# A three-stage macaron layer on one core: batches written out, side jobs spread over all sixteen slots, x2 begun on GpSimd

## The chip, the core and the metric

The kernel runs on one core of a Trainium2 chip. The metric is the device time of one execution in microseconds (us), the lower the better. The engines are TensorE (PE: matmuls; its weight loads are listed as PEld), VectorE (DVE), ScalarE (ACT), GpSimd (POOL) and SyncE (SP, which here only issues DMAs). Each runs its own list of instructions in order; semaphores tie them together.

## What is computed

Eight batches of 512 rows by 256 columns pass three steps, all in float32:

```python
x = x + 0.5 * ffn(layernorm(x), w_re, w_im, bias)
x = x + attn(layernorm(x), Wq, Wk, Wv, Wo, bo)
x = x + 0.5 * ffn(layernorm(x), w_re, w_im, bias)

def ffn(x, w_re, w_im, bias):      # FFT over 256, times a complex 256x256 matrix, inverse FFT
    y = real(ifft(fft(x) @ complex(w_re, w_im)))
    return y + bias

def attn(x, Wq, Wk, Wv, Wo, bo):   # only the left 128 columns enter; 16 heads of 8
    left = x[..., :128]
    q, k, v = (left @ W.T for W in (Wq, Wk, Wv))        # each (512, 16, 8)
    att = softmax(q k^T / 4)                            # 16 x 512 x 512 per batch
    return (att v) @ Wo.T + bo
```

## The kernel before, in words

The FFT, the matrix and the inverse FFT are linear, so a **prologue** folds them once into one real 256x256 matrix, `half_ffn`: six products with cosine and sine tables on TensorE (`spectral`, L504), put together on VectorE (`fold`, L859 and L860). After that each batch has a prefix, an attention and a suffix.

The **attention** of a batch is 16 *slots* (`QUADS`). In slot s TensorE makes the scores of four heads for one block of 128 keys, in two pairs (`score_pair`, L587: stationary `KS`, moving `QS`, 34 rows deep); ScalarE takes the exponent of each pair, 128x1024 at a time (L489); and `value_quad` (L606) multiplies `VS` with the four heads' `probs`, side by side in four column groups of the array, 32 wide each. The code issues the scores of slot s+1, then the `value_quad` of slot s, then the jobs of slot s. There are two score banks, so a pair waits until ScalarE has read the pair two before it. After slots 0 to 7 and 8 to 15 `normalize` (L778 to L789) divides by the sums of the exponents; its second call ends in `otn`.

Around these lie small **jobs** on TensorE, each evacuated by VectorE, in two shared PSUM banks (`misc`) in turn, so a job waits until the job two before it has been evacuated. The prefix of a batch is F1_0 to F1_3 (first FFN, four row tiles, L529, to `x1`), LT (transposes of the normalised left half `lh`, L561), KT, QT and V (projections), N and NT (a bound on the scores: squares on GpSimd, summed and transposed, L570 to L574). The suffix is WO_0 to WO_3 (output projection, added to `x2`), T3_0 and T3_1 (transposes of `x2`, L546) and F2_0 to F2_3 (second FFN, to `x_out`). `x2` begins as `x1` plus `bo` (`begin_x2`, L793, VectorE); `x_in` and `x_out` get the bias on GpSimd (`add_bias`, L409), and `rstd_of` (L404, L406) makes the reciprocal standard deviations there. Tables at the top of the file (`PREFIX`, `SUFFIX`) say in which slot a job goes: while batch b is in its slots, the suffix of b-1 and the prefix of b+1 are done.

`KT` and `QT` are split in two parts (`split`, L718 and L720, to `kp` and `qp`), **stored to DRAM and read back as stacked rows** (`stack_parts`, L312 to L332): 8 DMAs of 128 KB each for `KS` and 8 for `QS`, on SP. The `guard` reads one number on TensorE and VectorE (L613, L800); where it says that the scores are small, a long block is jumped over and the shift rows are zero. Four small DMAs then put them into `QS` (L340; L481 on ScalarE's queue for the first batch).

Batches 0 and 7 are written out; batches 1 to 6 are three rounds of a hardware loop of two batches on each engine. `keep_awake` (L511) are matmuls on zeros that fill waits of TensorE in the prologue and after the last batch.

## Time and profile before

| | us |
| --- | --- |
| time before, median of 3 runs | 401.53 (400.44 to 403.65) |
| the profiled execution | 399.26 |
| its span, first to last instruction | 397.5 |
| PE busy / ACT busy / DVE busy / POOL busy | 363.7 / 248.4 / 196.4 / 92.3 |
| granted TensorE clock, mean | 0.983 |

The span is shorter than the time of the same execution by what lies around the first and last instruction (1.8 us). Busy time of PE includes the modelled ends of pipelined matmuls, so 92% is not 92% of its peak. A slot is best read from the start of one `value_quad` to the start of the next in the PE timeline; a batch from the start of its slot 0 (47.43 us for batch 0, 83.24 for batch 1, 347.63 for batch 7).

### The profile page before, as it was taken

How to read it: one execution, taken by the hardware profiler on the slowest of the kernel's cores; microseconds unless marked ns; L12 is line 12 of the kernel's file. 1: busy time of each engine (PE TensorE's matmuls, PEld its weight loads, DVE VectorE, ACT ScalarE, POOL GpSimd, SP SyncE). 2: the span in 40 equal slices, each digit the busy share in tenths (PEclk: the TensorE clock that was granted, in tenths of full speed). 3: DMA queues.
4: the chain of work that ended last, by engine and by line, in shares of the span. 5: the costliest groups of instructions: out<-in, count | busy, mean ns of one | idle time of the engine just before them, and what ended most of it. 6: DMA issues, size and time to landing. Idle time of an engine off the chain costs nothing.

```text
span 397.5 us, 9585 instructions
## 1 busy us (share of the span) xinstructions
PE 363.7 (92%) x3436; PEld 142.1 (36%) x3441; DVE 196.4 (49%) x511; ACT 248.4 (62%) x261; POOL 92.3 (23%) x96
## 2 busy tenths in 40 slices
PE   5887599999999999899999999899999999999986
PEld 3734133233333333233333333233433333333323
DVE  1575243246645575156645575427554673333354
ACT  1100378967686767737676767736687667887730
POOL 6351120402430131302430141301530131003004
PEclk9999899999999999989999999969999999999999
DMA  8509939500874039230874039230781038200001
GB/s 220 160 0 230 202 115 162 156 2 2 197 132 160 2 128 178 81 109 2 200 129 160 2 140 177 68 108 2 186 142 54 2 128 178 77 2 2 27 28 53
DMA packets 19500, 40.75 MB, mean 103 GB/s; under 512 B 3504, under 2 KB 6064, under 8 KB 18416
## 3 DMA queue, kind: packets, MB, share of 16 engines
q1 hardware_dynamic: 17968, 39.27, 40.2%
q10 hardware_dynamic: 1472, 0.67, 0.8%
q8 instruction: 39, 0.64, 0.7%
q14 instruction: 21, 0.17, 0.2%
HBM read 26.69 MB, written 12.58 MB: 99 GB/s over the span
## 4 chain that ended last, share of the span: by engine, by line
PE 73%; issue 9%; ACT 8%; DVE 4%; DMA 3%; ACTq 2%; DVEq 0%; POOL 0%
PE ot L606 25%; PE misc L529 22%; PE scores L587 19%; ACT probs L489 8%; PE misc L546 2%; PE scores L504 2%; DMA cos_var_sb<-cos_var 2%; DMA QS<-shift 1%; PE misc L561 1%; ACTq L481 1%; PE scores L511 1%; DVE kp L718 1%; DVE kp L720 1%; DVE stats L689 0%; ACTq L266 0%
## 5 line engine op out<-in xcount | busy, mean ns | idle before, releaser
L489 ACT ACTIVATE probs<-scores 128x1024 f32<-128x1024 f32 x256 | 245.6, 1024 | 119.1 <-PE scores L587 118.9
L606 PE MATMUL ot<-probs,VS 128*32 128x512 f32 x1024 | 139.0, 615 | 0.3 <-ACT probs L489 0.3
L587 PE MATMUL scores<-QS,KS 34*128 34x512 f32 x512 | 105.3, 467 | 18.4 <-ACT probs L489 9.5
L587 PEld LDWEIGHTS scores<-QS,KS 34*128 34x128 f32 x512 | 42.4, 186 | 99.0 <-ACT probs L489 68.0
L404 POOL TENSOR_SCALAR veps<-mv 128x4 f32<-128x4 f32 (+1 forms) x25 | 6.6, 263 | 236.9 <-DVE mv L696 236.9
L744 DVE SCALAR_TENSOR_TENSOR x_out<-misc,rstd,x_out 128x256 f32<-128x256 f32 x32 | 15.5, 483 | 50.9 <-PE misc L529 50.7
L529 PE MATMUL misc<-half_ffn,xT_in 128*32 128x256 f32 x512 | 33.3, 397 | 3.6 <-issue 2.3
L606 PEld LDWEIGHTS ot<-probs,VS 128*32 128x32 f32 x1024 | 20.3, 108 | 42.4 <-issue 40.5
L529 PE MATMUL misc<-half_ffn,xT 128*32 128x256 f32 x512 | 33.0, 379 | 0.4 <-DVE xT L729 0.4
L735 DVE SCALAR_TENSOR_TENSOR x<-misc,rstd,x_in 128x256 f32<-128x256 f32 x32 | 15.5, 484 | 30.6 <-PE misc L529 30.2
L529 PEld LDWEIGHTS misc<-half_ffn,xT_in 128*32 128x32 f32 x512 | 17.6, 115 | 23.3 <-issue 13.7
L406 POOL TENSOR_TENSOR rstd<-veps,power 128x4 f32<-128x4 f32 (+1 forms) x25 | 25.3, 1011 | 2.1
L689 DVE BATCH_NORM_STATS2 stats<-x 128x6 f32<-128x256 f32 x64 | 25.1, 415 | 0.0
L529 PEld LDWEIGHTS misc<-half_ffn,xT 128*32 128x32 f32 x512 | 16.7, 110 | 23.2 <-issue 15.6
L729 DVE COPY xT<-misc 128x512 f32<-128x512 f32 x16 | 11.0, 691 | 22.7 <-PE misc L546 22.7
L739 DVE TENSOR_TENSOR x<-misc,x 128x256 f32<-128x256 f32 x32 | 13.5, 423 | 17.5 <-PE misc L529 17.4
L529 PE MATMUL misc<-wo_sb,otn 128*32 128x256 f32 x256 | 19.4, 380 | 0.8 <-DVE otn L789 0.7
L409 POOL TENSOR_TENSOR x_out<-x,half_bias 128x1024 f32<-128x1024 f32 (+1 forms) x9 | 19.1, 2127 | 0.0
L415 POOL TENSOR_TENSOR sq_k<-kp 128x512 bf16<-128x512 f32 x8 | 8.3, 1040 | 46.1 <-DVE kp L718 46.1
L409 POOL TENSOR_TENSOR x_in<-x_in,half_bias 128x1024 f32<-128x1024 f32 x8 | 19.0, 2377 | 0.0
L689 DVE BATCH_NORM_STATS2 stats<-x_in 128x6 f32<-128x256 f32 x32 | 11.2, 414 | 15.1 <-DMA x_in<-x 7.6
L778 DVE STREAM_TRANSPOSE ot_t<-ot 128x512 f32<-128x512 f32 x16 | 11.4, 710 | 13.4 <-PE ot L606 13.2
(77 smaller groups left out, 240.4 us busy)
## 6 DMA issues: line engine op xcount, KB each, us to landing
KS<-k_scr SPq DMA_DIRECT2D x64, 128.0 KB, 4.6
QS<-q_scr SPq DMA_DIRECT2D x64, 128.0 KB, 4.8
x_in<-x SPq DMA_DIRECT2D x8, 512.0 KB, 4.2
xT_in<-x_t SPq DMA_DIRECT2D x8, 512.0 KB, 4.9
k_scr<-kp SPq DMA_DIRECT2D x8, 512.0 KB, 2.7
q_scr<-qp SPq DMA_DIRECT2D x8, 512.0 KB, 3.4
out<-x_out SPq DMA_DIRECT2D x14, 256.0 KB, 2.1
out<-x_out SPq DMA_DIRECT2D x4, 128.0 KB, 1.9
```

The costliest lines, as they stand in the source:

```text
L406: nc.gpsimd.tensor_tensor(rstd[k][:, tiles], veps[k][:, tiles], power[:, tiles], ALU.pow).then_inc(rstd_done[k], 1)
L409: nc.gpsimd.tensor_tensor(dst[:, tiles, :], src[:, tiles, :], half_bias[:, :].unsqueeze(1).to_broadcast([P, tiles.stop - tiles.start, E]), ...
L489: nc.scalar.activation(probs[u % PRING][:, :, :], scores[u % 2][:, :, :], ACT.Exp, scale=SCORE_SCALE).then_inc(exp_done, 1)
L529: last = mm(dst[cols, :], lhsT[:, cols], rhs, start=c == 0, stop=c == len(terms) - 1)
L587: last = mm(scores[u % 2][:, i, :], KS[par][rows, slot, kt * P:(kt + 1) * P].bitcast(F32R), QS[par][rows, slot, :].bitcast(F32R), start=Tr ...
L606: last = mm(ot[g][COL * j:COL * (j + 1), :], VS[par][:, kt, h, :], probs[(2 * s + j // 2) % PRING][:, j % 2, :], start=s % 8 == 0, stop=s ...
L689: ins = nc.vector.bn_stats(stats[k][:, t, :], src[:, t, :])
L729: nc.vector.tensor_copy(xT[:, 2 * i:2 * i + 2, :, :], bank[:, :].rearrange("p (t c q) -> p t c q", t=2, c=C)).then_inc(evacuated, 1)
L735: nc.vector.scalar_tensor_tensor(x1[par][:, i, :], tile, rstd[0][:, i:i + 1], x_in[par][:, i, :], ALU.mult, ALU.add).then_inc(evacuated, 1)
L739: nc.vector.tensor_tensor(x2[:, i, :], tile, x2[:, i, :], ALU.add).then_inc(evacuated, 1)
L744: nc.vector.scalar_tensor_tensor(x_out[:, i, :], tile, rstd[2][:, i:i + 1], x_out[:, i, :], ALU.mult, ALU.add).then_inc(evacuated, 1)
L778: nc.vector.transpose(ot_t[:, :, :].rearrange("p c r -> p (c r)"), ot[g][:, :]).then_inc(ot_taken, 1)
```

## The change

The loop is gone: every engine's list is written out for all eight batches, and waits compare with constants. One table `STEADY` takes the place of `PREFIX` and `SUFFIX` (with `BEGIN` for batch 0 and `END` for batch 7). In it QT, V, N and NT belong to the next batch, but F1, LT and KT to the batch after that (+2). For this there are three `x1` buffers, the `left_half` (to `lh`) is written in slot 11, and `kp` is stored a batch ahead (`k_out`). `x2` is begun on GpSimd, after the previous batch's T3_1 and its `x_out`. The guard stands after the jobs of slot 10; the first `normalize` in slot 12.

`k_scr` is laid out as `q_scr` was, and rows in `KS` are ordered by part first; a `QS` DMA now writes 32 rows (256 KB) from a source read twice, so a batch has 8 DMAs for `KS` and 4 for `QS`.

In the prologue the cosine table with row 0 zeroed is loaded whole, and the plain low half (`cos_low`) after the bias on ScalarE's queue; the identity and small weights come on SP behind batch 0's `x`; `bo` and `wo` come last. The exponent table is loaded early by a small activation. NT of batch 0 stands ahead of V; of batch 1 only F1_0 and F1_1 are done there. The stacked rows of batch 0 are issued from SP and ScalarE, for the first eight slots; those for the last eight slots wait for `rest_wanted`, set by TensorE when it starts on the scores. After the last batch the transposes go to score banks and are copied by ScalarE, between the WO and F2 jobs.

```diff
-PREFIX = {0: ["F1_0", "F1_1"], 1: ["F1_2", "F1_3"], 3: ["LT"], 4: ["KT"], 5: ["QT"], 6: ["V"], 7: ["N"], 8: ["NT"]}
-SUFFIX = {3: ["WO_0"], 4: ["WO_1"], 5: ["WO_2"], 6: ["WO_3"], 8: ["T3_0"], 9: ["T3_1"],
-          11: ["F2_0"], 12: ["F2_1"], 13: ["F2_2"], 14: ["F2_3"]}
-GUARD_SLOT = 9
-NORM0_SLOT = 10
...
+STEADY = {0: [("QT", 1)], 1: [("V", 1)], 2: [("WO_0", -1), ("N", 1)], 3: [("WO_1", -1), ("NT", 1)],
+          4: [("WO_2", -1), ("WO_3", -1)], 5: [("T3_0", -1), ("T3_1", -1)],
+          6: [("F1_0", 2)], 7: [("F1_1", 2)], 8: [("F1_2", 2)], 9: [("F1_3", 2)],
+          10: [("F2_0", -1)], 11: [("F2_1", -1)], 12: [("F2_2", -1)], 13: [("F2_3", -1)],
+          14: [("LT", 2)], 15: [("KT", 2)]}
+BEGIN = {0: [("F1_2", 1)], 1: [("F1_3", 1)], 3: [("LT", 1)], 4: [("KT", 1)], 5: [("QT", 1)], 6: [("V", 1)],
+         7: [("N", 1)], 8: [("NT", 1), ("F1_0", 2)], 9: [("F1_1", 2)], 10: [("F1_2", 2)], 11: [("F1_3", 2)],
+         14: [("LT", 2)], 15: [("KT", 2)]}
+END = {2: [("WO_0", -1)], 3: [("WO_1", -1)], 4: [("WO_2", -1)], 5: [("WO_3", -1)], 6: [("T3_0", -1)],
+       7: [("T3_1", -1)], 9: [("F2_0", -1)], 10: [("F2_1", -1)], 11: [("F2_2", -1)], 12: [("F2_3", -1)]}
+GUARD_SLOT = 10
+LEFT_SLOT = 11
...
-        x1 = [sb(f"x1_{i}", [P, T, E]) for i in range(2)]
+        x1 = [sb(f"x1_{i}", [P, T, E]) for i in range(3)]
...
+        def k_rows(eng, par, g, side):
+            heads = slice(HEADS * side + 4 * g, HEADS * side + 4 * (g + 1))
+            for j in range(PARTS):
+                first = SIDE * side + PARTS * Dh * j
+                eng.dma_start(KS[par][first:first + PARTS * Dh, 4 * g:4 * (g + 1), :],
+                              k_scr[j, :, heads, :].unsqueeze(0).to_broadcast([PARTS, Dh, 4, S])).then_inc(rows_loaded[g], 16)
+
+        def q_rows(eng, par, g, side):
+            heads = slice(HEADS * side + 4 * g, HEADS * side + 4 * (g + 1))
+            eng.dma_start(QS[par][SIDE * side:SIDE * side + SROW, 4 * g:4 * (g + 1), :],
+                          q_scr[:, :, heads, :].rearrange("i d h s -> (i d) h s").unsqueeze(0)
+                          .to_broadcast([PARTS, PARTS * Dh, 4, S])).then_inc(rows_loaded[g], 16)
...
+            def first_rows():
+
+
+                sp.wait_ge(evacuated, evac_count("KT", 0))
+                store_k(sp)
+                sp.wait_ge(k_stored, 16)
+                k_rows(sp, 0, 0, 0)
+                sp.wait_ge(q_stored, 16)
+                q_rows(sp, 0, 0, 0)
+                sp.wait_ge(rest_wanted, 1)
+                for side in range(SIDES):
+                    k_rows(sp, 0, 1, side)
+                for side in range(SIDES):
+                    q_rows(sp, 0, 1, side)
...
+            def rows_in(b):
+                sp.wait_ge(evacuated, evac_count("QT", b))
+                store_q(sp)
+                wait(sp, quad_done, QUADS * (b - 1))
...
+            for it in range(B):
+                if it == 0:
+                    load_x(2)
+                    k_out(1)
+                if it + 1 < B:
+                    rows_in(it + 1)
+                if it + 3 < B:
+                    load_x(it + 3)
+                if it + 1 < B:
+                    shift_rows(it + 1)
+                if it >= 1:
+                    store_out(it - 1)
+                if it + 2 < B:
+                    k_out(it + 2)
...
+            def end_of(b):
+                rstd_of(2, b + 1)
+                wait(pool, out_stored, 32 * b)
+                add_row(x_out, x2, half_bias, x2b_done)
+
+            def begin_x2(b):
+
+                pool.wait_ge(evacuated, evac_count("F1_3", b))
+                if b >= 1:
+                    pool.wait_ge(evacuated, evac_count("T3_1", b - 1))
+                    pool.wait_ge(x2b_done, b)
+                add_row(x2, x1[b % 3], bo_sb, x2_begun)
+
...
+            for it in range(1, B):
+                if it + 1 < B:
                     square(qp, sq_q, qp_step, it + 1)
+                end_of(it - 1)
+                begin_x2(it)
+                if it + 2 < B:
+                    rstd_of(1, it + 3)
+                if it + 3 < B:
+                    next_x(it + 3)
+                if it + 2 < B:
+                    square(kp, sq_k, kp_step, it + 2)
+            pool.wait_ge(out_stored, 32 * (B - 1))
             for i in range(2):
+                pool.wait_ge(evacuated, evac_count(f"WO_{2 * i + 1}", B - 1))
+                add_row(x_out, x2, half_bias, x2b_done, slice(2 * i, 2 * i + 2))
                 rstd_of(2, B + i, slice(2 * i, 2 * i + 2))
...
+            act.wait_ge(waking_set, 1)
+            nc.scalar.activation(probs[0][:, 0, 0:32], waking[:, 0:32], ACT.Exp, scale=SCORE_SCALE)
...
+            act.wait_ge(k_stored, 16)
+            k_rows(act, 0, 0, 1)
+            act.wait_ge(evacuated, evac_count("QT", 0))
+            store_q(act)
+            act.wait_ge(q_stored, 16)
+            q_rows(act, 0, 0, 1)
             act.wait_ge(shift_ready, 1)
             for side in range(SIDES):
...
+            pe.sem_inc(rest_wanted, 1)
...
+            def last_transposes(i):
+                pe.wait_ge(evacuated, evac_count(f"WO_{2 * i + 1}", B - 1))
+                transpose_x2(scores[0][:, i, :], i).then_inc(lastT_ready, 1)
+
+            job("WO_0", B - 1)
+            job("WO_1", B - 1)
+            job("WO_2", B - 1)
+            last_transposes(0)
+            job("WO_3", B - 1)
+            job("F2_0", B - 1)
+            last_transposes(1)
+            job("F2_1", B - 1)
+            job("F2_2", B - 1)
+            job("F2_3", B - 1)
 
 
         @block.vector
         def _(dve):
...
+            def left_half(b):
+                dve.wait_ge(rstd_done[1], b + 1)
+                for t in range(T):
+                    last = nc.vector.tensor_scalar(lh[:, t, :], x1[b % 3][:, t, 0:HD], mv[1][:, t, 0:1],
+                                                   rstd[1][:, t:t + 1], ALU.subtract, ALU.mult)
...
-            def begin_x2(par):
-
-                nc.vector.tensor_tensor(x2[:, :, :], x1[par][:, :, :], bo_sb[:, :].unsqueeze(1).to_broadcast([P, T, E]),
-                                        ALU.add).then_inc(x2_begun, 1)
-
...
+            for it in range(B):
                 for s in range(QUADS):
-                    if s == 0 and not is_first(it):
-                        begin_x2(1 - par)
+                    if s == 0 and it >= 1:
                         normalize(it - 1, 1)
-                    run_jobs(it, par, s)
-                    if s == 9:
+                    run_jobs(it, s)
+                    if s == 2 and it == 0:
+                        left_half(1)
+                    if s == 5 and it == 0:
+                        norm0_stats(2)
+                        norm_moments(0, 3)
+                    if s == GUARD_SLOT and it + 1 < B:
+                        guard(it + 1)
+                    if s == LEFT_SLOT and it + 2 < B:
+                        left_half(it + 2)
+                    if s == 12:
                         normalize(it, 0)
-                    if s == GUARD_SLOT and not is_last(it):
-                        guard(it + 1)
-                    if s == NORM0_SLOT and tail:
-                        norm0_moments(it + 2, par)
-
-            body(0, 0)
-            with dve.Fori(1, B - 3, 2) as i:
-                body(i, 1)
-                body(i + 1, 0)
-            for it in range(B - 3, B):
-                body(it, it % 2, tail=it + 2 < B)
-            dve.wait_ge(evacuated, ring_base(EPILOGUE))
-            begin_x2((B - 1) % 2)
+                    if s == 13 and it + 3 < B:
+                        norm0_stats(it + 3)
+                        norm_moments(0, it + 4)
```

**TensorE, batches in the middle.** First the kernel before, slots 2 and 3 of a batch (`wo_sb,otn` is WO, `ident,lh` is LT):

```order
L606 MATMUL ot<-probs,VS 32x512 x4
L266 REGISTER_ALU
L587 MATMUL scores<-QS,KS 128x512 x2
L266 REGISTER_ALU
L587 MATMUL scores<-QS,KS 128x512 x2
L606 MATMUL ot<-probs,VS 32x512 x4
L266 REGISTER_ALU
L529 MATMUL misc<-wo_sb,otn 32x256 x4
L266 REGISTER_ALU x2
L561 MATMUL misc<-ident,lh 128x128 x4
```

and slots 2 and 3 after the change (`sq` rows are N, `ident,norms` is NT):

```order
L629 MATMUL ot<-probs,VS 32x512 x4
L546 MATMUL misc<-wo_sb,otn 32x256 x4
L594 MATMUL misc<-sq_q,head_ones 32x512
L595 MATMUL misc<-sq_k,head_ones 32x512
L611 MATMUL scores<-QS,KS 128x512 x4
L629 MATMUL ot<-probs,VS 32x512 x4
L546 MATMUL misc<-wo_sb,otn 32x256 x4
L598 MATMUL misc<-ident,norms 1x64
L611 MATMUL scores<-QS,KS 128x512 x4
```

Slot 2 had nothing between its `value_quad` and the next scores; now it has WO_0 and N, and the register instructions are gone.

**VectorE, the turn of a batch.** Before, where a batch begins (`x_0` is x1):

```order
L793 TENSOR_TENSOR x<-x_0,bo_sb 128x1024
L266 ISA
L778 STREAM_TRANSPOSE ot_t<-ot 128x512
L266 ISA
L780 RECIPROCAL recip<-ot_t 128x32
L266 ISA
L783 TENSOR_TENSOR on<-ot_t,recip 128x16x16
L266 REGISTER_ALU
L789 STREAM_TRANSPOSE otn<-on 128x512
L266 ISA
L266 REGISTER_ALU
L735 SCALAR_TENSOR_TENSOR x_0<-misc,rstd,x_in 128x256
```

and after the change:

```order
L751 CAST kp<-misc 128x512
L753 TENSOR_TENSOR kp<-misc,kp 128x512
L810 STREAM_TRANSPOSE ot_t<-ot 128x512
L812 RECIPROCAL recip<-ot_t 128x32
L815 TENSOR_TENSOR on<-ot_t,recip 128x16x16
L821 STREAM_TRANSPOSE otn<-on 128x512
L751 CAST qp<-misc 128x512
L753 TENSOR_TENSOR qp<-misc,qp 128x512
L791 COPY VS<-misc 128x32x8 x2
L775 TENSOR_TENSOR x<-misc,x 128x256
L796 TENSOR_REDUCE norms<-misc 64x1
```

`begin_x2` is gone from this place; KT's split stands ahead of the four instructions of `normalize`, QT's split and V's copy behind them, and then the first WO and N.

**ScalarE's list in the prologue.** Before:

```order
L472 COPY even<-scores 128x258 x2
L475 ACTIVATE even<-scores 128x258
L475 ACTIVATE odd<-scores 128x258
L481 DMA QS<-shift 1x8x512 x4
L489 ACTIVATE probs<-scores 128x1024 x32
```

and after:

```order
L487 ACTIVATE odd<-scores 128x258
L277 DMA KS<-k_scr 16x1x2048 x2
L270 DMA q_scr<-qp 128x2x512
L282 DMA QS<-q_scr 32x1x2048
L289 DMA QS<-shift 1x8x512 x4
L504 ACTIVATE probs<-scores 128x1024 x256
```

Two `KS` DMAs, the store of `qp` and one `QS` DMA now stand ahead of the four shift DMAs in this list, and the store of `qp` behind the two `KS` DMAs.

## Rows read from the trace of the kernel before

**Rows 1.** Busy time by stretch: batches 0, 1, 6 and 7 (columns in the first line).

```profile
core 0: us, PE busy (x) PEld busy (x) DVE busy (x) ACT busy (x) POOL busy (x), PEclk, DMA share, GB/s
47.43:83.24 35.81, 33.97 (x251) 10.59 (x249) 11.82 (x27) 30.09 (x33) 6.58 (x5) 0.96 0.58 135
83.24:125.86 42.62, 41.12 (x418) 15.72 (x417) 24.35 (x65) 30.73 (x33) 10.59 (x10) 1.00 0.43 91
...
305.13:347.63 42.50, 41.20 (x418) 15.73 (x416) 22.40 (x56) 30.72 (x33) 6.95 (x7) 1.00 0.35 90
347.63:381.11 33.48, 32.07 (x283) 11.16 (x281) 10.47 (x24) 28.19 (x30) 3.61 (x3) 1.00 0.05 17
```

**Rows 2.** Busy time by stretch, one slot each, around batch 4.

```profile
212.73:215.12 2.39, 1.97 (x15) 0.53 (x13) 2.28 (x4) 2.39 (x3) 0.00 (x0) 1.00 0.58 158
218.50:221.88 3.38, 3.38 (x46) 1.49 (x44) 1.64 (x5) 1.94 (x3) 0.00 (x0) 1.00 0.00 0
...
226.95:229.90 2.95, 2.95 (x30) 0.97 (x28) 1.81 (x4) 1.95 (x3) 0.00 (x0) 1.00 0.00 0
...
236.11:238.49 2.38, 2.13 (x17) 0.64 (x15) 1.52 (x6) 2.38 (x3) 1.96 (x3) 1.00 0.66 195
238.49:240.93 2.44, 2.44 (x20) 0.95 (x18) 0.75 (x2) 1.43 (x3) 1.64 (x1) 1.00 0.75 134
...
243.31:245.55 2.24, 1.97 (x14) 0.53 (x12) 1.40 (x4) 2.06 (x3) 0.00 (x0) 1.00 1.07 158
245.55:248.08 2.53, 2.53 (x31) 0.98 (x29) 1.82 (x9) 1.69 (x3) 0.00 (x0) 1.00 1.06 186
```

**Rows 3.** PE timeline inside the last of these slots (start, duration, line).

```profile
246.44 1.05 PE L529 MATMUL misc<-half_ffn,xT 128*32 128x256 f32 x16
247.41 0.73 PE L587 MATMUL scores<-QS,KS 34*128 34x512 f32 x4
```

**Rows 4.** Busy time by stretch: two slots at the end of batch 0.

```profile
79.20:83.24 4.04, 3.76 (x27) 1.06 (x25) 1.04 (x2) 3.76 (x5) 0.00 (x0) 1.00 0.00 0
```

**Rows 5.** PE timeline at the loop's jump back before batch 3.

```profile
169.59 1.22 PE L587 MATMUL scores<-QS,KS 34*128 34x512 f32 x4 [2.15 <-issue]
```

**Rows 6.** PE timeline of the prologue (in brackets idle time before, and what ended it).

```profile
1.19 3.60 PE L511 MATMUL ot<-waking 128*128 128x512 bf16 x8 [1.19 <-DVE waking L863]
7.83 0.80 PE L504 MATMUL scores<-cos_var_sb,wre_sb 128*128 128x129 f32 x2 [3.05 <-DMA cos_var_sb<-cos_var]
...
17.25 3.66 PE L529 MATMUL misc<-half_ffn,xT_in 128*32 128x256 f32 x64 [1.34 <-DVE half_ffn L860]
...
44.18 0.73 PE L587 MATMUL scores<-QS,KS 34*128 34x512 f32 x4 [2.02 <-DMA QS<-shift]
```

**Rows 7.** Busy time by stretch in the prologue.

```profile
7.80:10.00 2.20, 2.17 (x10) 2.17 (x11) 0.24 (x1) 0.04 (x1) 0.88 (x1) 1.00 1.05 382
12.30:14.00 1.70, 1.70 (x16) 1.70 (x16) 0.19 (x2) 0.37 (x1) 1.70 (x2) 1.00 1.11 322
...
35.80:39.50 3.70, 3.65 (x60) 2.15 (x60) 2.12 (x5) 0.00 (x0) 0.00 (x0) 1.00 1.01 192
```

**Rows 8.** DVE timeline: the last instruction of KT's split.

```profile
28.74 0.69 DVE L720 TENSOR_TENSOR kp<-misc,kp 128x512 fp32r<-128x512 f32 x1
```

**Rows 9.** ACT timeline: the issues of the shift rows of batch 0.

```profile
35.80 3.41 ACTq L481 DMA_DIRECT2D QS<-shift  x4
```

**Rows 10.** DMA issues from 29 to 45 us (KB each, median us to landing).

```profile
KS<-k_scr SPq DMA_DIRECT2D x8, 128.0 KB, 4.6
...
k_scr<-kp SPq DMA_DIRECT2D x1, 512.0 KB, 2.7
```

**Rows 11.** PE and DVE timeline of the tail.

```profile
386.88 2.76 PE L511 MATMUL scores<-waking 128*128 128x512 bf16 x11
...
394.67 0.48 DVE L744 SCALAR_TENSOR_TENSOR x_out<-misc,rstd,x_out 128x256 f32<-128x256 f32 x1 [0.38 <-PE misc L529]
```

**Rows 12.** DVE and POOL timeline: end of `normalize`, and the bias of `x_in`.

```profile
215.47 0.71 DVE L789 STREAM_TRANSPOSE otn<-on 128x512 f32<-128x512 f32 x1
...
249.62 2.39 POOL L409 TENSOR_TENSOR x_in<-x_in,half_bias 128x1024 f32<-128x1024 f32 x1
```

More of the change, by code:

```diff
@@ new lines, with slots_of @@
+PROLOGUE, EPILOGUE = -1, B
+def slots_of(it):
+    if it == PROLOGUE:
+        return {0: [(f"F1_{t}", 1) for t in range(T)], 1: [("LT", 1)],
+                2: [("KT", 1), ("QT", 1), ("N", 1), ("NT", 1)], 3: [("V", 1), ("F1_0", 2), ("F1_1", 2)]}
+    if it == EPILOGUE:
+        return {0: [(f"{kind}_{t}", -1) for kind in ("WO", "F2") for t in range(T)]}
+    table = BEGIN if it == 0 else END if it == B - 1 else STEADY
+    return {s: [(name, d) for name, d in jobs if it + d < B] for s, jobs in table.items()}
@@ L117, in quad_units, with evac_count, jobs_at @@
+ORDER = [(it, s, name, it + d) for it in range(PROLOGUE, EPILOGUE + 1)
+         for s, jobs in sorted(slots_of(it).items()) for name, d in jobs]
+INDEX = {(name, b): n for n, (_, _, name, b) in enumerate(ORDER)}
+def evac_count(name, b):
+    return INDEX[name, b] + 1
+def jobs_at(it, s):
+    return [(name, b) for at, slot, name, b in ORDER if (at, slot) == (it, s)]
 def quad_units(s):
@@ L262, in wait @@
         def wait(eng, s, value):
[L264 to L282 removed]
+            if value > 0:
+                eng.wait_ge(s, value)
@@ L446, in _ @@
[L446 to L452 removed]
+            square(kp, sq_k, kp_step, 1)
+            square(qp, sq_q, qp_step, 1)
+            next_x(2)
+            pool.wait_ge(late_loaded, 32)
+            begin_x2(0)
+            rstd_of(1, 3)
+            next_x(3)
+            square(kp, sq_k, kp_step, 2)
@@ L490, in body @@
                                          scale=SCORE_SCALE).then_inc(exp_done, 1)
-            iterations(act, body)
+            for i in range(2):
+                act.wait_ge(lastT_ready, i + 1)
+                nc.scalar.copy(xT[:, 2 * i:2 * i + 2, :, :],
+                               scores[0][:, i, :].rearrange("p (t c q) -> p t c q", t=2, c=C)).then_inc(lastT_copied, 1)
         @block.tensor
@@ L833, in run_jobs, with last_jobs @@
                         norm_moments(k, b + 1)
-                        if kind == "F1" and not (static(it) and it == PROLOGUE):
-                            norm_apply(1, src, lh, HD, b + 1)
-            def last_suffix():
-                b, jobs, base = B - 1, [job[1] for job in LAST], ring_base(EPILOGUE)
-                def take(name):
-                    evacuate(name, jobs.index(name), base, b, b % 2, EPILOGUE)
+            def last_jobs():
+                b = B - 1
                 for i in range(2):
```

526 lines of the change are left out of this document (218 added, 308 removed).

## The prediction

> **What bounds the kernel now.** I read the page first (TensorE is busy 92% of the span), then the busy time by stretch, batch by batch, then the TensorE timeline slot by slot. A batch in the middle takes 42.5 to 42.6 us, while batch 0 takes 35.8 and batch 7 takes 33.5 [rows 1]: those two carry fewer jobs. The slots tell why. A slot with one F2 job lasts 2.53 us, with TensorE busy for all of it [rows 2]; the job itself takes 0.97 us, from its start to the next scores [rows 3], so **scores and values alone are 1.56 us of TensorE work**. Two F1 jobs make 3.38 [rows 2], so 0.91 each. WO and KT together make 2.95 [rows 2]; KT has F2's size (0.97), which leaves 0.42 for WO. T3 and NT add 0.88 [rows 2].
>
> An empty slot lasts 2.39, not 1.56, with ScalarE busy throughout; the N slot 2.38 [rows 2]. There TensorE waits for two exponents. Where several light slots follow one another, as at the end of batch 0, two last 4.04, so 2.02 each [rows 4]. Hence the limit of a slot: the larger of TensorE's work and about 2.0 us, or 2.4 for the first light slot after full ones. **Each empty slot between full ones wastes 0.8 us of TensorE.** The guard stands in an otherwise empty slot of 2.24 [rows 2]: 1.56 plus 0.68, covered by the exponents only in part.
>
> Batches 1 to 6 last 347.63 - 83.24 = 264.4 us [rows 1], against 6 x 42.5 = 255.0 for clean ones. The other 9.4 us lie mostly at the loop's two jumps back, where TensorE idles 2.15 us for nothing but instructions [rows 5], and then does the next jobs more slowly. At the ends, scores start at 44.18, after a wait for the shift rows [rows 6], and the last result is written at 394.67 + 0.48 = 395.15 [rows 11], 14 us after the last values.
>
> **Middle batches (1 to 5).** By the new table, with the prices above: QT and V slots 2 x 2.53; WO_0 with N 2.38 (N's slot alone is 2.38 by ScalarE's limit [rows 2], and I take it that WO's 0.42 fits into TensorE's wait there); WO_1 with NT 2.2; WO_2 with WO_3 2.5; both T3 2.9; four F1 slots 4 x 2.53, single ones priced as F2; F2_0 with the guard 1.56 + 0.97 + 0.68 = 3.2, since a job there no longer lets exponents cover the guard; three F2 slots 7.6; LT 2.4 (light, between full ones); KT 2.53. Sum 40.9, so -1.7 for a batch, **-8.5 for five**. If the guard's read hides behind the queued F2 matmuls, it is -2.2 a batch.
>
> **Batch 6** has no F1, LT and KT any more: four empty slots in a row, 2.38 + 3 x 2.02, take the place of four at 2.53, and slots 14 and 15 become 2.38 and 2.02. That is 38.7, or **-3.8** against 42.5. Empty slots still cost 2 us each, which is why the work it loses (some 5.4 us) does not all come back.
>
> **Batch 0** takes that work: six F1, LT and KT of batch 2. Slots by the same prices, the first 1.2 longer, since TensorE starts at the lower clock (batch 0 has 0.96 granted on the mean, and 0.04 of 35.8 us is 1.4): 3.7, 2.53, 2.38, 2.27, 3 x 2.53, 2.3, 2.73, 2.53, 3.2, 2.53, 2.38, 2.02, 2.27, 2.53. Sum 41.0, so **+5.2**. **Batch 7** keeps its jobs, each moved by a slot: 0.
>
> **The loop** goes, and with it its 9.4 us: **-9.4**. Batches 0 and 7 are written out already and show slots of the same length as in the loop, so the register instructions that go too are worth nothing.
>
> **Prologue.** The first product waits for the third table until 7.83; the waking matmuls before it take 3.60 for eight [rows 6]. Now only the first table is needed, which lands earlier, and nine waking matmuls end at about 5.2: -2.6. From 7.80 to 10.00 ten matmul rows take 2.2 us, from 12.30 to 14.00 sixteen take 1.7 [rows 7], about twice as fast, although the granted clock is printed as 1.00 in both (the level of 2.4 GHz). TensorE had idled 3.05 us before the slow ones [rows 6]; without that gap I take most of them at the fast rate, -1.6 more. So F1 starts at 13.0 instead of 17.25 [rows 6], and KT's split, which ends at 28.74 + 0.69 = 29.43 [rows 8], at 25.2. If they stay slow, it is only -2.4. The store of `kp` lands 2.7 later [rows 10], 27.9. Now SP and ScalarE issue two `KS` DMAs each, and ScalarE the store of `qp` behind its two (28.8); queued behind their data it lands at about 33, and the two `QS` DMAs, with 4.6 us as for a `KS` DMA [rows 10], at 37.6. The shift DMAs follow in ScalarE's list: four took 3.41 us to issue, from 35.80 [rows 9], and the last was waited for until 44.18, behind the rows for both halves. The second half's rows now come after, so the last shift row should land 1 to 2 us after its issue: **38.2, so -6.0**. V and two F1 fit into that time and cost nothing. Bounds: 35 (-9), if `qp` is stored as fast as `kp`; 44 (0), if rows take as long as before.
>
> Here a rule weighs against the change. From 35.80 to 39.50 the DMA engines are full (share 1.01) at 192 GB/s [rows 7]: the queue is not what is short. The Trainium skill ("Trainium Kernel Development and Optimization", Key Constraints) says that DMAs of all queues run on the same 16 engines and that issuing from several saves only issue time; the trace agrees. By that rule alone, three issues fewer in a row would be all the gain, some 1.5 us on top of the earlier start. My sum does not rest on two queues, but on half the rows being left for later.
>
> **Tail.** Eleven waking matmuls, 2.76 us [rows 11], fill the time until the last sums of `x2` are normalised, then come transposes, copies and all F2. Now the first half's transposes go ahead of WO_3, ScalarE copies them, F2_0 follows. VectorE still has its 4 sums, 4 statistics and 4 results; I get the last result at 392.4 in the old time, **-2.7** (bounds 0 and -3.5).
>
> **x2 on GpSimd.** VectorE loses one pass a batch, which TensorE never waited for: 0. GpSimd gains one pass of 2.4 us, the length of the `x_in` pass [rows 12], between slots 6 and 9; WO needs it eight slots later: 0. With the cover gone it would be 2.4 a batch. The `KS` and `QS` rows of a batch are issued from slot 0 instead of slot 5, and the shift rows one job later, still three slots ahead of use: 0. Four `QS` DMAs fewer on SP: 0.
>
> **Sum.** -8.5 - 3.8 + 5.2 - 9.4 - 6.0 - 2.7 = **-25.2**. The profiled execution took 399.26, so 374.1. It lies 2.3 below the median of the three runs shown and 1.2 below the lowest. I add half of the 2.3 and round up, since plans with tight turns seldom lose nothing: **376**.
>
> **Rivals.**
>
> 1. *The turn of a batch becomes a chain.* Before, `normalize` ended at 216.18 [rows 12], 2.6 us after the last values, with only F1 behind it. Now KT's split stands ahead of it, QT's split and V's copy behind it; WO_0 needs QT's bank, N needs V's and GpSimd's square of QT. From the start of slot 15's values: values 0.9, KT 0.97, its split 1.4 (2 x 0.69 [rows 8]), `normalize` 2.3, QT's split 1.4, so 7.0; WO_0 is due after three slots and the values, 2.53 x 3 + 0.9 = 8.5. That leaves 1.5, and with V's copy 0.9 before N. GpSimd's pass over `x_in`, 2.39 us [rows 12], ends just before. If it comes late by over 0.9 us, TensorE waits 1 to 2.4 us in each of six batches: +6 to +14, so 382 to 390. The Trainium skill ("SBUF — State Buffer", "SBUF: two separate sides") has a rule for it: a VectorE instruction with two SBUF inputs and a GpSimd one that reads SBUF lock each other out for the whole instruction. In `normalize` the product of `ot_t` and `recip` is such an instruction; no row here shows it beside a GpSimd pass.
> 2. *The rows come no sooner.* The DMA engines are full, and the store of `qp` is beside and behind four `KS` DMAs: scores start near 43, +5: 381.
> 3. *Written-out code is slower.* If TensorE's instructions were fetched too slowly wherever no loop repeats them, each block would cost what the jump back costs, 2.15 us idle [rows 5] and as much again for the slow jobs after. It decides from seven blocks on, 7 x 4 = 28 us; with ten it is +40 - 25, so 416. Against it: batches 0 and 7 are written out, and no slot there waits for instructions.
> 4. *More than forecast:* rows at 35, the guard hidden: 376 - 3 - 2.5 = 370.
>
> **Chances.** Forecast 0.58 (own range 372 to 380.5), rival 1 0.18, rival 2 0.11, rival 4 0.09, rival 3 0.04. The range for 8 in 10 is 369 to 386: it leaves out rival 3, the upper part of rival 1 and little below. About 1% (4 us) is what the runs of this kernel can tell from no change. Faster by over 1% needs under 397.5: all cases but rival 3, 0.95. Within 1%: 0.01. Slower: 0.04.
>
> **What would show each step.** Slots of a middle batch: 40.9 us from slot 0 to slot 0, no slot empty, slot 10 about 3.2, no idle time of TensorE before WO_0 and N in slot 2. Batch 0 near 41, batch 6 near 38.7, no idle for instructions above 0.7. F1 at 13.0, scores at 38.2, the last result 11.3 us after the last values start. The forecast is wrong if the idle time before TensorE's WO, N or LT jobs comes back in each batch with VectorE or GpSimd as its cause, or if middle batches stay above 42.

## The result, and the profile after

The changed kernel takes **526.18 us** (median of 4 executions, 525.09 to 527.34) against 401.02 for the kernel before in the same comparison: a ratio of 1.311, 95% interval 1.304 to 1.317. The forecast was 376 with a range of 369 to 386, so both the size and the sign are wrong. Where the executions of a kernel fell into a faster and a slower group, the time given below is that of the faster one. The profiled execution took 527.34, with a span of 525.5 and a mean granted clock of 0.844 (before: 0.983).

The page of the profile after, sections 1 to 3: busy time of each engine, the span in 40 slices, the DMA queues.

```profile
PE 369.9 (70%) x3424; PEld 141.6 (27%) x3428; DVE 178.2 (34%) x494; ACT 251.7 (48%) x264; POOL 110.3 (21%) x104
...
PE   7840698500999169952999089933998399719996
...
PEclk9995599855899769995899669985999599955999
DMA  8121413131214212230213211320212021210011
...
q1 hardware_dynamic: 14298, 38.35, 20.6%
...
KS<-k_scr SPq DMA_DIRECT2D x62, 128.0 KB
QS<-q_scr SPq DMA_DIRECT2D x31, 256.0 KB
x_in<-x SPq DMA_DIRECT2D x8, 512.0 KB, 29.6
```

No engine has added work that would explain 125 us: TensorE is busy for 369.9 us against 363.7, ScalarE for 251.7 against 248.4, GpSimd for 110.3 against 92.3 (`x2`), VectorE for less. TensorE stands still in a hole once a batch, and after each hole the clock is low. The DMA line looks idle, with 1 to 3 tenths in most slices. Yet an `x_in` load takes 29.6 us from issue to landing (median); in the kernel before it took 4.2. Full queues and idle-looking engines at the same time are what has to be explained.

Idle time of TensorE, grouped by what it waited for (us in total, times, longest):

```profile
PE scores L611 <- issue: 104.6, 6, 31.5
PE scores L611 <- DMA QS<-shift: 33.7, 2, 20.0
```

All eight large waits stand before the first scores of a batch. The jobs that rival 1 feared for (WO, N) wait for nothing in the middle batches. Busy time by stretch, from slot 0 to slot 0: batches 0, 1, 2, 6, 7, with the columns of [rows 1].

```profile
59.56:136.65 77.09, 42.81 (x359) 14.46 (x357) 21.50 (x62) 30.14 (x33) 14.15 (x13) 0.75 0.25 82
136.65:194.48 57.83, 42.38 (x418) 16.14 (x416) 21.79 (x62) 31.07 (x33) 13.05 (x12) 0.85 0.25 84
194.48:252.46 57.98, 42.45 (x419) 16.14 (x417) 21.70 (x62) 31.07 (x33) 12.99 (x12) 0.85 0.23 84
422.13:474.52 52.39, 38.12 (x343) 13.60 (x341) 14.61 (x37) 30.82 (x33) 7.83 (x6) 0.86 0.19 73
474.52:511.53 37.01, 35.93 (x282) 11.86 (x281) 9.35 (x24) 28.55 (x30) 5.99 (x4) 0.87 0.04 15
```

The hole of batch 1, in the PE timeline, and the stretches around it (slot 14's wait, slot 15, the next slot 0):

```profile
188.74 1.22 PE L611 MATMUL scores<-QS,KS 34*128 34x512 f32 x4 [15.45 <-issue]
189.90 1.93 PE L629 MATMUL ot<-probs,VS 128*32 128x512 f32 x8
191.60 1.93 PE L546 MATMUL misc<-leftT,wk_sb 128*32 128x512 f32 x8
```

```profile
171.64:187.00 15.36, 1.65 (x14) 0.58 (x12) 0.38 (x2) 1.82 (x2) 0.00 (x0) 0.68 0.23 87
...
189.90:194.48 4.58, 4.58 (x22) 1.09 (x20) 0.84 (x2) 1.79 (x3) 2.41 (x2) 0.52 0.00 0
194.48:197.00 2.52, 2.52 (x22) 0.72 (x21) 2.42 (x5) 1.89 (x3) 0.94 (x1) 1.00 0.44 171
```

After 15.45 us without work TensorE is granted 0.52 of its full clock (the level of 1.2 GHz) for the 4.58 us of slot 15, which has KT; the next slot, with as many matmuls for QT, takes 2.52 once 1.00 is granted again. So a hole costs its length and some 2.1 us more. The label "issue" is to be read with care: the matmul waits for the rows and the shift rows together, and nothing on an engine released it. The issues of SP tell the rest:

```profile
141.36 2.52 SPq L277 DMA_DIRECT2D KS<-k_scr  x4
143.93 1.31 SPq L282 DMA_DIRECT2D QS<-q_scr  x2
145.28 4.23 SPq L277 DMA_DIRECT2D KS<-k_scr  x4
149.56 7.01 SPq L282 DMA_DIRECT2D QS<-q_scr  x2
156.61 4.51 SPq L297 DMA_DIRECT2D x_in<-x  x1
161.16 0.43 SPq L298 DMA_DIRECT2D xT_in<-x_t  x1
164.70 8.39 SPq L289 DMA_DIRECT2D QS<-shift  x4
```

All of these are issued by 173.1, and the first scores start at 188.74, 47.4 us after the first row was issued. A busy stretch in between, with nothing but stacked rows under way:

```profile
150.00:155.00 5.00, 5.00 (x52) 2.33 (x54) 1.77 (x3) 3.68 (x5) 4.66 (x4) 1.00 0.12 52
```

**DMA share 0.12 of 16 engines is two engines, both full.** The packet records of the trace show the same: two packets are in flight for 4.89 of these 5 us, and three for 0.10. They move 52 GB/s here (55 and 56 in the stretches on either side). The rows of a batch are 8 x 128 KB and 4 x 256 KB, 2.1 MB: 37 us at 56 GB/s. Behind them in the same queue come `x_in`, `xT_in` and last the shift rows, of which these two engines carry their part as well. The packets show it: 112 of the 128 packets of `x_in` move between 161 and 165 us; the last row packet ends at 184.98, the last two engines' share of `x_in`, 16 packets, at 186.2, and the last of the shift rows at 189.15. Rows can be issued only after QT's split and store in slot 0, 10.3 us after the first scores (131.07 to 141.36), and 47.4 later come the next ones: 57.7 a batch, all of it set by the two engines and what precedes them.

Why two: in the change each stacked-row DMA has the two copies as its outermost dimension (`unsqueeze(0).to_broadcast([PARTS, ...])`, PARTS = 2). The Trainium skill ("DMA: Bandwidth & Descriptors", "Rules for kernel authors", the row "Use all 16 engines") says that the slowest dimension that is not of size 1 sets how many engines take part, and that a leading broadcast of c copies, with c under 16, confines the DMA to at most c. The traces agree: two packets in flight with the two copies outermost, and in experiment 3, with 8 rows outermost and no broadcast, eight.

### The profile page after: what moved, and what is told of

The parts are those of the page before. It is cut to its first block, busy times and chain, and to the rows that moved or that the text cites. A ratio compares the mean times of both kernels' runs of the same rounds, so it can differ in the third digit from the quotient of the medians.

```text
span 525.5 us, 8688 instructions
## 1 busy us (share of the span) xinstructions
PE 369.9 (70%) x3424; PEld 141.6 (27%) x3428; DVE 178.2 (34%) x494; ACT 251.7 (48%) x264; POOL 110.3 (21%) x104
## 4 chain that ended last, share of the span: by engine, by line
PE 55%; issue 20%; DMA 19%; DVE 2%; SPq 1%; ACT 1%; ACTq 1%; POOL 0%; DVEq 0%; PEldq 0%
PE ot L629 21%; PE misc L546 16%; PE scores L611 15%; DMA QS<-q_scr 8%; DMA QS<-shift 6%; DMA q_scr<-qp 2%; PE misc L552 1%; DMA cos_low_sb<-cos_low 1%; DMA k_scr<-kp 1%; ACT probs L504 1%; SPq L277 1%; PE misc L585 1%; ACTq L277 0%; PE scores L521 0%; ACTq L289 0%
## 5 line engine op out<-in xcount | busy, mean ns | idle before, releaser
L629 PE MATMUL ot<-probs,VS 128*32 128x512 f32 x1024 | 146.5, 646 | 0.3 <-ACT probs L504 0.3
L611 PEld LDWEIGHTS scores<-QS,KS 34*128 34x128 f32 x512 | 44.5, 203 | 213.4 <-issue 161.6
L780 DVE SCALAR_TENSOR_TENSOR x_out<-misc,rstd,x_out 128x256 f32<-128x256 f32 x32 | 15.5, 483 | 49.5 <-PE misc L546 49.5
L771 DVE SCALAR_TENSOR_TENSOR x<-misc,rstd,x_in 128x256 f32<-128x256 f32 x24 | 11.6, 484 | 39.7 <-PE misc L546 39.7
L546 PEld LDWEIGHTS misc<-half_ffn,xT_in 128*32 128x32 f32 x512 | 16.5, 112 | 25.1 <-issue 14.7
L546 PEld LDWEIGHTS misc<-half_ffn,xT 128*32 128x32 f32 x512 | 16.4, 110 | 23.5 <-issue 17.1
L751 DVE CAST kp<-misc 128x512 fp32r<-128x512 f32 x8 | 5.5, 692 | 41.1 <-PE misc L546 41.1
L407 POOL TENSOR_TENSOR x<-x,bo_sb 128x1024 f32<-128x1024 f32 x8 | 19.1, 2382 | 1.2 <-DVE x L771 0.8
## 6 DMA issues: line engine op xcount, KB each, us to landing
x_in<-x SPq DMA_DIRECT2D x8, 512.0 KB, 29.6
```

The lines of the kernel that those rows point to most:

```text
L407: nc.gpsimd.tensor_tensor(dst[:, tiles, :], src[:, tiles, :], row[:, :].unsqueeze(1).to_broadcast([P, tiles.stop - tiles.start, E]), ALU.a ...
L546: last = mm(dst[cols, :], lhsT[:, cols], rhs, start=c == 0, stop=c == len(terms) - 1)
L611: last = mm(scores[u % 2][:, i, :], KS[b % 2][rows, slot, kt * P:(kt + 1) * P].bitcast(F32R), QS[b % 2][rows, slot, :].bitcast(F32R), star ...
L629: last = mm(ot[g][COL * j:COL * (j + 1), :], VS[b % 2][:, kt, h, :], probs[(2 * s + j // 2) % PRING][:, j % 2, :], start=s % 8 == 0, stop= ...
L771: nc.vector.scalar_tensor_tensor(x1[b % 3][:, i, :], tile, rstd[0][:, i:i + 1], biased[:, i, :], ALU.mult, ALU.add).then_inc(evacuated, 1)
L780: nc.vector.scalar_tensor_tensor(x_out[:, i, :], tile, rstd[2][:, i:i + 1], x_out[:, i, :], ALU.mult, ALU.add).then_inc(evacuated, 1)
```

## The experiments

**1. The rows as before, all else as in the change.** The decisive one.

```diff
-    k_scr = nc.dram_tensor("k_scr", [PARTS, Dh, H, S], ...)
+    k_scr = nc.dram_tensor("k_scr", [H, Dh, PARTS, S], ...)
...
-                              k_scr[j, :, heads, :].unsqueeze(0).to_broadcast([PARTS, Dh, 4, S]))
+                              k_scr[heads].rearrange("h d j s -> (d j) h s"))
...
-            eng.dma_start(QS[par][SIDE * side:SIDE * side + SROW, ...], q_scr[...].unsqueeze(0).to_broadcast(...))
+            for j in range(PARTS):
+                eng.dma_start(QS[par][first:first + SROW:PARTS, ...], q_scr[:, :, heads, :].rearrange("i d h s -> (i d) h s"))
```

The order of the heads in `wk_t` and `head_ones`, the store of `kp` and the counts that are waited for go back with the layout.

> The changed kernel with only the stacked rows loaded as before: k_scr laid out by head, 8 DMAs of 16 rows for KS and 8 of 16 rows for QS a batch (outermost dimension 16 in each), instead of 8 and 4 whose outermost dimension is the two copies. Theory A (a DMA runs on as many of the 16 DMA engines as its outermost dimension has entries, so on two; the changed kernel shows a DMA share of 0.12 to 0.13 for 15 us and more a batch): the waits of 11 to 31 us before the scores in slot 15 vanish, the DMA share during the rows goes to 0.6 and above, scores start at 38 to 40, time 372 to 380. Theory B (the new order on SP is at fault: x is loaded between the rows and the shift rows, which then come late whatever their shape): at least 8 us of wait stay in each batch, time above 450. Theory C (written-out code is at fault): no change, 520 to 530.

Measured: 371.63 us (371.06 to 372.37), ratio to the kernel before 0.924 [0.920, 0.929]. These DMAs have 16 rows outermost. The whole loss comes from the way the rows are loaded, and the rest of the change is worth some 30 us. Shape, count and layout of the row DMAs were put back together here; experiments 3 and 4 keep the layout of the change. TensorE's line in section 2 of its page, and its stretches (batches 0, 1, 6, 7, and 92 to 104 us, in which the rows of a batch move):

```profile
PE   8776499999999999999999999999999999999986
```

```profile
44.82:86.38 41.56, 40.14 (x359) 13.76 (x357) 21.77 (x62) 30.16 (x33) 12.78 (x13) 0.95 0.57 144
86.38:126.20 39.82, 39.82 (x419) 15.60 (x417) 21.90 (x62) 31.02 (x33) 13.68 (x12) 1.00 0.52 122
...
285.48:322.63 37.15, 36.32 (x342) 13.27 (x340) 14.78 (x37) 30.89 (x33) 8.08 (x6) 1.00 0.47 103
322.63:355.95 33.32, 32.07 (x282) 11.16 (x281) 9.63 (x25) 28.46 (x30) 5.97 (x4) 1.00 0.05 17
```

```profile
92.00:104.00 12.00, 12.00 (x124) 4.91 (x118) 6.24 (x20) 9.38 (x11) 3.92 (x4) 1.00 1.05 190
```

The same bytes move at 190 GB/s with all engines busy, in some 12 us, and TensorE has no idle time at all in a middle batch (39.82 of 39.82).

**2. The same edit alone, in the kernel before.** `k_scr`, `KS` and `QS` as the change has them, nothing else.

```diff
-                                         k_scr[heads].rearrange("h d j s -> (d j) h s")).then_inc(rows_loaded[g], 16)
+                                         k_scr[i, :, heads, :].unsqueeze(0).to_broadcast([PARTS, Dh, 4, S])).then_inc(rows_loaded[g], 16)
...
+                                     q_scr[:, :, heads, :].rearrange("i d h s -> (i d) h s").unsqueeze(0)
+                                     .to_broadcast([PARTS, PARTS * Dh, 4, S])).then_inc(rows_loaded[g], 16)
```

> The kernel before with only the rows loaded as in the change (outermost dimension two; k_scr laid out as q_scr). Theory A: about 36 us for the rows of a batch, which here are issued from slot 5 on and wanted in slot 15, 25 us later, so 12 to 25 us of wait in each of eight batches: 500 to 600. Theories B and C: unchanged, 397 to 404.

Measured: 610.18 us (two executions, 609.82 and 610.55), ratio 1.518 [1.510, 1.527]; above the 500 to 600 expected. Waits of TensorE:

```profile
PE scores L586 <- DMA QS<-shift: 175.9, 7, 26.2
PE scores L586 <- DMA QS<-q_scr: 17.4, 1, 17.4
```

In the kernel before, the rows are issued five slots later, so less of their time is covered: up to 26.2 us a batch stay open, where the change leaves 15.5. The earlier issue, which I priced at 0, softens the fault. The row shape is enough by itself to make the kernel before slow.

**3. Each copy as its own DMA, in the change's layout.** `K` DMAs with 8 rows outermost, `Q` DMAs with 16.

```diff
-                              k_scr[j, :, heads, :].unsqueeze(0).to_broadcast([PARTS, Dh, 4, S]))
+                for i in range(PARTS):
+                    eng.dma_start(KS[par][first + Dh * i:first + Dh * (i + 1), ...], k_scr[j, :, heads, :])
```

`QS` is loaded as in experiment 4.

> The changed kernel with its layout and row order, but each copy of the rows in a DMA of its own: 16 DMAs of 8 rows (64 KB) for KS and 8 of 16 rows (128 KB) for QS a batch. Source bytes are still read twice. Theory A (engines by outermost dimension): 8 and 16 engines, so the DMA share is about 0.5 during KS and near 1 during QS, rows of a batch in 10 to 12 us, all hidden, time 372 to 382. Rival D (it is the repeated source that is slow, since two copies read the same DRAM rows): the copies still meet there, rows stay slow, time above 450. More DMAs on SP: 24 x 0.45 to 0.6 us of issue, some 13 us a batch, hidden.

Measured: 393.44 and 394.06 us (two more executions took 399.40 and 400.54), where 372 to 382 was expected: the direction is right, the size missed. The number of engines is as expected. In the prologue, while nothing but `KS` rows of these DMAs is under way (29.4 to 30.4 us), eight packets are in flight for 0.81 us and nine for 0.16, the 4-byte writes among them. There is no broadcast in these DMAs, so it is the outermost size that shows here, and not the repeated dimension. Waits of TensorE, and one of them with the job ahead of it:

```profile
PE scores L613 <- issue: 13.2, 6, 4.0
PE scores L613 <- DMA QS<-shift: 6.7, 1, 6.7
```

```profile
165.01 1.05 PE L548 MATMUL misc<-half_ffn,xT 128*32 128x256 f32 x16
168.00 0.74 PE L613 MATMUL scores<-QS,KS 34*128 34x512 f32 x4 [1.95 <-issue]
```

This wait is not one for rows. It stands behind F2_0 in slot 10, where the guard's read and jump are, and these scores (slot 12) wait for no DMA. The same wait comes in batches 1 to 4 (1.36, 1.95, 2.23 and 1.83 us), and with the slot after it, which in two of them runs at a lower clock, it makes all of the 10.7 us by which these four batches are longer than in experiment 1. Batches 5 and 6 are as short as there. The rest of the 22 us lies in batch 0 (10.0 longer, with waits of 3.95 and 1.90 at its end) and ahead of it (1.6). An `x_in` load lands after 15.1 to 16.9 us, and the DMA engines are full until the guard's slot:

```profile
107.00:115.00 8.00, 8.00 (x80) 3.56 (x80) 4.80 (x18) 5.93 (x7) 3.51 (x3) 1.00 1.00 114
161.00:165.00 4.00, 4.00 (x42) 1.50 (x44) 2.18 (x8) 2.94 (x4) 0.00 (x0) 1.00 1.02 120
```

Rows and `x_in` move at 114 GB/s here with a full share, where experiment 1 had 190, and so they are not done when the guard comes. Five of the six waits labelled "issue" (all but the 1.90) end 3.3 to 3.5 us after a 16 KB packet of the instruction queue (q8) began, which took 1.66 to 1.78 us each time. The longest (3.95, before 86.20) comes after the first of a slot's four score matmuls, inside a pair, where the code has no wait at all. That TensorE's code comes late through full DMA engines would explain them. This is argued and not shown: packets as long (281.24, 321.38) also pass without a wait. Why the rows move so slowly stays open as well; that 16 `K` DMAs of 64 KB run beside 8 of `Q` may have to do with it.

**4. Only Q split, K with its two copies outermost.** A rung between the change and experiment 3.

```diff
-            eng.dma_start(QS[par][SIDE * side:SIDE * side + SROW, ...], ... .to_broadcast([PARTS, PARTS * Dh, 4, S]))
+            for j in range(PARTS):
+                eng.dma_start(QS[par][first:first + PARTS * Dh, ...], q_scr[:, :, heads, :].rearrange("i d h s -> (i d) h s"))
```

> The changed kernel with only its QS DMAs undone: each copy of q is a DMA of its own whose outermost dimension is 16 rows; the KS DMAs keep their outermost pair of copies. Theory (a DMA works on as many engines as its outermost dimension is long): the KS half, 1 MB a batch, moves on 2 engines at the 52 to 57 GB/s seen before, 18 to 20 us, and the QS half on 16 in about 5 us; 24 us fit into the 39.8 of a batch, so the waits of 15 us in middle batches go or shrink below 4, and the prologue's scores start near 46. Time 374 to 395, DMA share 0.12 to 0.13 only while KS moves. Rival (the repeated reading of one source or the zero stride itself is slow, whatever stands outermost): QS would read the same source twice as before and stay slow, time above 450.

Measured: 431.10 us (428.50 to 433.74), ratio 1.075 [1.070, 1.080]. The rival that rereading a source is slow would need over 450 and falls, but the 374 to 395 of the theory fall as well. (The rival had the zero stride in it too; no DMA of this run repeats `q` by a zero stride, so that half of it rests on experiment 3.) A stretch with only `KS` rows left, and one of the middle waits:

```profile
136.00:142.00 6.00, 6.00 (x68) 2.24 (x68) 2.48 (x10) 4.78 (x5) 1.26 (x2) 1.00 0.14 55
```

```profile
200.62 1.22 PE L612 MATMUL scores<-QS,KS 34*128 34x512 f32 x4 [4.81 <-issue]
```

The `K` rows go at 55 GB/s on two engines as expected (two packets in flight for 3.98 of the 6 us, three for 1.98). My expectation added the two halves (24 us) and forgot the queue: the two slow engines have to work off their part of `QS`, `x_in` and `xT_in` too before they reach the shift rows. `x_in` lands after 24.4 us (median), the shift rows behind it, and 3.9 to 4.8 us a middle batch stay open. **What counts is when the slowest engine reaches the last DMA of the queue, not the mean share.**

**5. The kernel before, with its loop written out.**

```diff
-            with dve.Fori(1, B - 3, 2) as i:
-                body(i, 1)
-                body(i + 1, 0)
+            for i in range(1, B - 3):
+                body(i, i % 2)
```

The loops of the other engines are written out in the same way.

> The kernel before with the loops of all engines written out, nothing else. The forecast's term: the jumps back and the slow jobs after them go, -9.4 us, so 390 to 393 in the old time of 399 to 401. Theory C (written-out code is slow to fetch): slower than before, 415 or more.

Measured: 391.48 us (390.00 to 392.55), ratio 0.975 [0.970, 0.980], 10.5 less than the median of before. The loop's term (-9.4) and the price of a clean batch both hold:

```profile
183.93:226.22 42.29, 41.05 (x419) 15.73 (x417) 24.17 (x64) 30.63 (x33) 10.58 (x10) 1.00 0.47 115
```

Rival 3 (written-out code fetched too slowly) is out.

**6. x2 back on VectorE**, from the kernel of experiment 1.

```diff
-                add_row(x2, x1[b % 3], bo_sb, x2_begun)
+                nc.vector.tensor_tensor(x2[:, :, :], x1[b % 3][:, :, :], bo_sb[...].to_broadcast([P, T, E]), ALU.add).then_inc(x2_begun, 1)
```

The pass stands in slot 0 again, ahead of `normalize`.

> The kernel with the rows as before (371.6 us), and the pass x1 plus bo moved back from GpSimd to VectorE, 1.22 us a batch in slot 0 ahead of normalize, as the kernel before had it. Forecast's term (x2 on GpSimd is worth 0): 371 to 372.5. Rival (with KT, QT and V at the turn of a batch VectorE has no room there; QT's split would end 1.2 us later than 130.6 in a batch whose WO_0 is due at 131.9, and V's copy at 132.7 before an N due at 132.3): TensorE waits 0.4 to 1 us in each of 6 batches, 374 to 378.

Measured: 374.63 us (374.28 to 375.14), ratio 0.932 [0.929, 0.935] against 0.924 [0.920, 0.929]: 3.0 us slower. The timelines of POOL, DVE and PE up to slot 2 show where:

```profile
127.18 1.05 POOL L414 TENSOR_TENSOR sq_k<-kp 128x512 bf16<-128x512 f32 x1
127.37 1.95 DVE L876 TENSOR_TENSOR x<-x,bo_sb 128x1024 f32<-128x1024 f32 x1
...
132.14 0.69 DVE L744 TENSOR_TENSOR qp<-misc,qp 128x512 fp32r<-128x512 f32 x1
...
132.89 0.64 PE L537 MATMUL misc<-wo_sb,otn 128*32 128x256 f32 x8 [0.22 <-DVE qp L744]
```

```profile
131.61:134.53 2.92, 2.68 (x24) 0.70 (x22) 2.79 (x6) 1.93 (x3) 1.04 (x1) 1.00 0.26 102
```

WO_0 waits 0.22 us for QT's split to free its bank, and its slot takes 2.92 instead of 2.30. Slot 2 is longer in batches 1 to 6, by 0.38, 0.62, 0.62, 0.62, 0.60 and 0.24, together 3.1. The chain of rival 1 exists, with VectorE's extra pass ahead of it. That pass costs more than the 1.22 us that it takes alone (356.67, in batch 7): in the four batches where GpSimd's square of `kp` starts just before, it takes 1.94 or 1.95, the rest of the square and 1.22 more. In batch 1 it started first, and the square took 2.04 instead of 1.04. The two passes took turns, as the rule in rival 1 has it, though in another instruction than the one named there. Moving the pass to GpSimd keeps it off the path.

**7. ScalarE stores `qp` before its two `KS` DMAs**, from the kernel of experiment 1.

```diff
-            act.wait_ge(k_stored, 16)
-            k_rows(act, 0, 0, 1)
             act.wait_ge(evacuated, evac_count("QT", 0))
             store_q(act)
+            act.wait_ge(k_stored, 16)
+            k_rows(act, 0, 0, 1)
             act.wait_ge(q_stored, 16)
```

> The kernel with the rows as before (371.6 us), and ScalarE's store of qp issued as soon as QT is split, ahead of its two KS DMAs and their wait for the store of kp. Theory (the late start of the scores, 41.6 instead of the 38.2 forecast, comes from the store of qp being issued at 29.2, 2.2 us after its data is there, and landing behind the KS rows, 5.7 us later): the store is issued at 27.0 and lands by 31, QS rows are issued there, scores start at 37 to 38.5; total 367.5 to 369, ratio to the kernel before 0.914 to 0.918. Rival (the DMA engines are full then, so the order among the DMAs moves nothing): scores stay at 41 to 42, total 371 to 372.

Measured: **366.30 us** (364.77 to 367.54), ratio 0.911 [0.908, 0.915]: the fastest version, and a little better than expected. In experiment 1 the store, the `QS` rows behind it and the first scores stood so:

```profile
29.17 0.44 ACTq L270 DMA_DIRECT2D q_scr<-qp  x1
...
34.85 1.49 ACTq L284 DMA_DIRECT2D QS<-q_scr  x2
...
41.57 0.73 PE L612 MATMUL scores<-QS,KS 34*128 34x512 f32 x4 [4.12 <-DMA QS<-shift]
```

and here:

```profile
26.40 0.39 ACTq L270 DMA_DIRECT2D q_scr<-qp  x1
...
29.24 1.49 ACTq L284 DMA_DIRECT2D QS<-q_scr  x2
...
37.01 0.73 PE L612 MATMUL scores<-QS,KS 34*128 34x512 f32 x4 [1.05 <-DMA QS<-shift]
```

The store lands 2.8 us after its issue when nothing is ahead of it, and 5.7 behind four `KS` DMAs.

**8. The guard's read ahead of slot 10's F2 job**, from the kernel of experiment 7.

```diff
                     value_quad(it, s)
+                    if s == GUARD_SLOT and it + 1 < B:
+                        maxima(it + 1, ...)
                     run_jobs(it, s)
-                    if s == GUARD_SLOT and it + 1 < B:
-                        maxima(it + 1, ...)
```

> The fastest version so far (rows as before, store of qp first, 366.3 us), with the guard's read and branch placed ahead of slot 10's F2 job instead of behind it, on TensorE and VectorE, so that only the value matmuls are queued ahead of it. Theory (the forecast's 0.68 us for the guard was no cost of its own: TensorE's sequencer reads ahead while queued matmuls run, and needs only some such work ahead of it): slot 10 stays at 2.52 and the time at 366 to 367. Rival (it hides only behind a queued F2 job of about 1 us beside the values): slot 10 takes 2.8 to 3.2 in each of 7 batches, 368 to 371.

Measured: 367.06 us (365.11 to 368.48), ratio 0.913 [0.909, 0.916]; no difference from experiment 7 that can be told.

```profile
145.96:148.53 2.57, 2.57 (x31) 0.95 (x29) 1.18 (x7) 1.93 (x3) 1.26 (x2) 1.00 0.03 6
```

Slot 10 takes 2.57 here with the guard ahead of its job; over batches 0 to 6 it takes 2.51 to 2.78, 2.59 on the mean. Behind the job it takes 2.52 in each, as long as a slot with F2 and no guard. So the guard has next to no price of its own as long as matmuls are queued and the DMA engines are idle, as they are in these runs (share 0.03). In experiment 3, with the engines full until then, the slot with the guard took 3.96 to 4.83 in batches 1 to 4.

## Why the prediction was wrong, and where it was right

The step that failed is "The `KS` and `QS` rows of a batch are issued from slot 0 instead of slot 5 ...: 0. Four `QS` DMAs fewer on SP: 0", and with it the prologue's "two `QS` DMAs, with 4.6 us as for a `KS` DMA [rows 10]". I counted the DMAs and their bytes, and carried over the landing time of another shape. The 4.6 us belonged to a DMA with 16 rows outermost. What the runs showed in place of the 0: the rows of a batch took 43.6 us from the first issue (141.36) to the last packet (184.98), on two engines, TensorE stood still for 15.1 to 15.8 us at the turn of a middle batch, and with 16 rows outermost all of that was gone (experiment 1). No rival was built on it: I asked whether rows are hidden, never how long they take in their new form. The rule of the Trainium skill that I weighed in its place ("Trainium Kernel Development and Optimization", Key Constraints: all queues share the 16 engines) agrees with [rows 7], a share of 1.01 while SP and ScalarE both had DMAs under way, and is beside the point, since it says nothing on how many of them one DMA uses.

The other terms can be read from experiment 1, whose profiled span is 370.3 against 397.5, so -27.2; forecast was -25.2. Starts of slot 0 give each term:

| step | forecast | measured |
| --- | --- | --- |
| start of batch 0 (47.43 to 44.82) | -6.0 | -2.6 |
| batch 0 (35.81 to 41.56) | +5.2 | +5.8 |
| batches 1 to 5, with the loop (221.9 to 199.1) | -17.9 | -22.8 |
| batch 6 (42.50 to 37.15) | -3.8 | -5.4 |
| batch 7 (33.48 to 33.32) | 0 | -0.2 |
| after batch 7 (16.4 to 14.4) | -2.7 | -2.0 |

- *Prologue.* F1 started at 13.0 in the changed kernel, as forecast. The rest was late: the store of `qp` landed at 34.8, not 33, and the four shift DMAs, issued from 36.38, took 3.2 us to issue and the scores started at 41.57, not 38.2. Experiment 7 shows that the order on ScalarE's queue was worth 4.6 us, more than the 3.4 missing.
- *Middle batches.* 39.82 instead of 40.9. The guard's slot took 2.52, not 3.2: its 0.68 had been worked out as 2.24 minus 1.56, but the exponents alone hold an empty slot that long (2.39 without the guard, [rows 2]); experiment 8 gives it 0.07 on the mean. T3 (2.68), LT and N (2.30) came out 0.1 to 0.2 below their prices as well.
- *Batch 6* gains from the same slots, the guard's above all.
- *Loop, batch 7, tail:* right within about a microsecond (the loop: 10.5 in experiment 5, for 9.4).
- *x2 on GpSimd:* priced at 0 from VectorE's side; against leaving it on VectorE it is worth 3.0 (experiment 6).
- *Rivals.* 1 did not come about in the change, but is one VectorE pass away. 3 is refuted. Rival 4's 370 is near what the change gives once the rows are put right. That experiment 1's 371.6 lies inside the forecast's range is in part luck: the start of batch 0 gained 3.4 less than forecast, batches 1 to 5 with the loop 4.9 more.

From experiment 1's span to the changed kernel's are 155.2 us: 14.7 before slot 0 of batch 0, 35.5 in batch 0, 86.4 in batches 1 to 5, 15.2 in batch 6, 3.7 in batch 7 (its first slots at 0.50 of the clock), -0.4 after. The waits at the seven turns (118.3) and the later start (14.7) make most of it; slots at the lower clock after the waits make some 17 of the other 22, and the rest was not taken apart.
